# Per-head exponentials with the maximum as bias in a fused stack of eight parts, and the order lists that go with them

## What is computed

```python
x = x + tanh(g_xattn[0]) * L0_xattn(ctx, layernorm(x), mask, mask)   # l0a: 8 heads of 16, 64 keys, masked
x = x + tanh(g_ffn[0])   * L0_ffn(layernorm(x))      # l0f0, l0f1: two layers of local attention and GLU
x = x + tanh(g_xattn[1]) * L1_xattn(layernorm(x), ctx)               # l1a: product, patches picked by position
x = x + tanh(g_ffn[1])   * L1_ffn(layernorm(x))      # l1f: 8 experts of rank 16, top 2
x = x + tanh(g_xattn[2]) * L2_xattn(ctx, layernorm(x), mask)         # l2a: 8 heads of 16, 64 keys, masked
x = x + tanh(g_ffn[2])   * L2_ffn(layernorm(x))      # l2f, l2g: ternary weights, rounded activations
x = x + tanh(g_xattn[3]) * L3_xattn(layernorm(x), ctx)               # l3a: 16 heads of 8, 64 given and 64 own keys
x = x + tanh(g_ffn[3])   * L3_ffn(layernorm(x))      # l3f, l3g: ternary, convolution over 3 rows, silu
# in each of the two layers of L0_ffn:
q = l2norm(q) * qs; k = l2norm(k) * ksc; q, k = rotary_xpos(q, k)
attn = softmax(8 * q @ k.T, causal within 64 rows); o = attn @ v     # 8 heads of 64
```

## Time and profile before

| | us |
|---|---|
| median of 3 runs | 1541.98 (1537.93 to 1543.62) |
| the profiled execution | 1545.68 |
| its span | 1543.9 |
| TensorE, TensorE weight load busy | 1372.6, 951.6 |
| VectorE busy | 1358.0 |
| ScalarE busy | 1019.0 |
| GpSimd busy | 753.3 |

### The profile page before, as it was taken

How to read it: one execution, slowest core, us unless ns; L and a number is a source line. 1 busy time by engine, 2 the same in 40 slices (tenths; PEclk the granted TensorE clock), 3 DMA queues, 4 the chain that set the end, 5 groups by cost and what they waited for, 6 DMA issues and landing times.

```text
span 1543.9 us, 42177 instructions
## 1 busy us (share of the span) xinstructions
PE 1372.6 (89%) x16206; PEld 951.6 (62%) x16206; DVE 1358.0 (88%) x4054; ACT 1019.0 (66%) x2037; POOL 753.3 (49%) x1147
## 2 busy tenths in 40 slices
PE   4888999989999899998988999899899989998877
PEld 2557656666566666575666656576566666666644
DVE  5878999889988899998989898989899999998875
ACT  1465778676766666776766766776676677666554
POOL 6676354545635355446446435735544553552310
PEclk9999999999999999999999999999999999999978
DMA  7001211111101121111211111122111021110110
GB/s 224 10 15 52 71 22 29 29 46 45 41 18 38 45 45 46 35 38 31 62 26 43 44 32 45 21 55 47 33 41 38 21 58 37 36 41 19 52 30 6
DMA packets 131000, 64.38 MB, mean 42 GB/s; under 512 B 97642, under 2 KB 123626, under 8 KB 130545
## 3 DMA queue, kind: packets, MB, share of 16 engines
q1 hardware_dynamic: 128209, 56.56, 14.8%
q10 hardware_dynamic: 2592, 5.12, 0.9%
HBM read 50.06 MB, written 2.14 MB: 34 GB/s over the span
## 4 chain that ended last, share of the span: by engine, by line
PE 50%; DVE 23%; ACT 14%; POOL 7%; issue 4%; DMA 1%; SPq 1%; POOLq 1%; DVEq 0%
PE ps_all L1442 8%; PE ps_all L1506 4%; PE ps_all L1731 4%; PE ps_all L1565 4%; PE ps_all L1480 3%; DVE mx L1121 3%; PE ps_all L1435 3%; PE ps_all L1519 3%; ACT L814 2%; PE ps_all L1551 2%; POOL wide_a L601 2%; PE ps_all L1687 2%; DVE wide_b L1124 2%; POOL rden L601 2%; POOL rstd L601 2%
## 5 line engine op out<-in xcount | busy, mean ns | idle before, releaser
L601 POOL TENSOR_TENSOR rstd<-rstd,minus_half 128x1 f32<-128x1 f32 x320 | 187.4, 592 | 595.2 <-DVE rstd L1099 590.8
L601 POOL TENSOR_TENSOR rden<-rden,minus_half 128x16 f32<-128x16 f32 x64 | 190.8, 2981 | 9.4
L601 POOL TENSOR_TENSOR wide_a<-wide_a,wide_b 128x256 f32<-128x256 f32 x256 | 181.5, 740 | 0.5 <-DVE wide_b L1178 0.4
L1121 DVE TENSOR_REDUCE mx<-ps_all 128x8 f32<-128x512 f32 (+1 forms) x192 | 164.7, 860 | 18.4 <-PE ps_all L1468 6.0
L852 ACT COPY wide_a<-ps_all 128x512 f32<-128x512 f32 (+1 forms) x192 | 138.3, 727 | 58.6 <-PE ps_all L1442 33.5
L1442 PE MATMUL ps_all<-ident,wide_b 128*128 128x128 f32 x1024 | 156.3, 285 | 14.7 <-ACT wide_b L865 5.7
L1442 PEld LDWEIGHTS ps_all<-ident,wide_b 128*128 128x128 f32 x1024 | 117.0, 145 | 52.4 <-issue 15.7
L814 ACT ACT_TABLE_LOAD x115 | 147.5, 1283 | 2.0
L865 ACT ACTIVATE wide_b<-wide_b 128x512 f32<-128x512 f32 (+1 forms) x160 | 113.9, 715 | 47.4 <-DVE wide_b L1124 46.3
L1506 PE MATMUL ps_all<-w_qkv,ht_shift 128*128 128x512 f32 x256 | 125.7, 614 | 6.6 <-DVE wide_b L1124 3.3
L1124 DVE TENSOR_TENSOR wide_b<-ps_all,mx 128x512 f32<-128x512 f32 (+1 forms) x160 | 126.3, 790 | 2.1
(11 more groups left out here) (266 smaller groups left out, 3611.8 us busy)
## 6 DMA issues: line engine op xcount, KB each, us to landing
wide_a<-in_k SPq DMA_DIRECT2D x64, 256.0 KB, 3.2
wide_c<-wide_c SPq DMA_DIRECT2D x128, 64.0 KB, 2.2
v_pad<-in_v SPq DMA_DIRECT2D x32, 256.0 KB, 4.1
v_pair<-in_v SPq DMA_DIRECT2D x32, 136.0 KB, 2.7
ctx_t<-in_ctx_t SPq DMA_DIRECT2D x32, 128.0 KB, 2.7
ctx_s<-in_ctx SPq DMA_DIRECT2D x32, 128.0 KB, 3.2
xin<-in_x SPq DMA_DIRECT2D x32, 64.0 KB, 2.6
mask_row<-in_mask_f SPq DMA_DIRECT2D x32, 64.0 KB, 3.0
```

The costliest lines, as they stand in the source:

```text
L601: return gp.tensor_tensor(o, a, b, op)
L1121: v.tensor_reduce(most, of, AX.X, ALU.max).then_inc(*done(f"{n}_max"))
```

## The change

- In the four attentions of 64 keys the subtraction is gone. The maximum of each head, negated, is the bias of a per-head exponential that reads the scores' banks itself: eight instructions of 128x64 on ScalarE for one of 128x512. The banks' reader is now the exponential. For l0a the factor 0.25 moves into `w_tgt` and `b_q` in the setup.
- In the two layers only the keys are scaled by their norm. Queries are transposed unscaled from `wide_a` as soon as the rotation is added, and the queries' inverse norm is the scale of the exponential. A new stage `less` on VectorE multiplies maximum by inverse norm by -1 (128x8). GpSimd raises keys' and queries' sums apart (8 columns each), the queries' behind the rotation.
- `w_gate` and `w_a` are one tensor of 136 columns and one product. The value product of l3a is one over all 128 rows; the second batch's given rows are laid on the other half of the partitions, so the third load is four DMAs for two, and L1335 becomes two instructions.
- `ORDER` and `BANK_TABLE` are new throughout; their entries are left out here. The new lists hold 3442 turns for VectorE (3506 before), 704 for GpSimd (640), and the same number for the others.

```diff
--- before.py
+++ after.py
@@ STAGES, ORDER and BANK_TABLE @@
     "dve": """
-        l0a_st l0a_var l0a_eps l0a_y l0a_k l0a_qs l0a_max l0a_sub l0a_inv l0a_o l0a_x l0f_st l0f_var l0f_eps
-        l0f_y l0f0_den l0f0_turned l0f0_qkn l0f0_max l0f0_sub l0f0_inv l0f0_o l0f0_y1 l0f0_st l0f0_var
+        l0a_st l0a_var l0a_eps l0a_y l0a_k l0a_qs l0a_max l0a_inv l0a_o l0a_x l0f_st l0f_var l0f_eps l0f_y
+        l0f0_den l0f0_turned l0f0_qkn l0f0_max l0f0_less l0f0_inv l0f0_o l0f0_y1 l0f0_st l0f0_var l0f0_eps
...
     "pool": """
-        l0a_rstd l0a_part l0f_rstd l0f0n_rstd l0f0_rot l0f0_one l0f0_rstd l0f1n_rstd l0f1_rot l0f1_one
-        l0f1_rstd l1a_rstd l1f_rstd l2a_rstd l2f_rstd l2f_xb l3a_rstd l3f_rstd
+        l0a_rstd l0a_part l0f_rstd l0f0k_rstd l0f0_rot l0f0q_rstd l0f0_one l0f0_rstd l0f1k_rstd l0f1_rot
+        l0f1q_rstd l0f1_one l0f1_rstd l1a_rstd l1f_rstd l2a_rstd l2f_rstd l2f_xb l3a_rstd l3f_rstd
...
-l0a_sc 45621615304040511251022563062660 2 l0a_sub
+l0a_sc 62600365506204043053055032164333 2 l0a_exp
...
-l0f0_sc 45010523316401340640322422032363 2 l0f0_sub
+l0f0_sc 65530123065533541213200020503151 2 l0f0_exp
...
@@ -368,8 +368,8 @@
         g_init = sb("g_init", [P, D])
-        w_gate = sb("w_gate", [P, E])
-        w_a = sb("w_a", [P, E * R])
+        w_experts = sb("w_experts", [P, E * R + E])
+        w_a, w_gate = w_experts[:, 0:E * R], w_experts[:, E * R:E * R + E]
@@ -580,10 +580,12 @@
                     sp.wait_ge(signal("l3a1_pv", (i - VALUES) % G), reached("l3a1_pv", i - VALUES))
-                sp.dma_start(k_part[:, s].rearrange("p (n k) -> p n k", n=8)[:, :, 0:ROW], d["k3"][i]).then_inc(
-                    signal(f"third_in{s}"), 16)
-                sp.dma_start(v_pad[0:64, i % VALUES].rearrange("p b h e -> p (b h e)"), d["v3"][i]).then_inc(
-                    signal(f"third_in{s}"), 16)
+                for b in range(2):
+                    far_half = slice(ROW - ROW * b, P - ROW * b)
+                    sp.dma_start(k_part[:, s].rearrange("p (b j k) -> p b j k", b=2, j=4)[:, b, :, far_half],
+                                 d["k3"][i][:, 4 * b:4 * b + 4, :]).then_inc(signal(f"third_in{s}"), 16)
+                    sp.dma_start(v_pad[far_half, i % VALUES, b].rearrange("p h e -> p (h e)"),
+                                 d["v3"][i][:, HID * b:HID * b + HID]).then_inc(signal(f"third_in{s}"), 16)
@@ -750,6 +752,14 @@
                     tt(rstd[:, s:s + 1], rstd[:, s:s + 1], minus_half[:, 0:1], ALU.pow).then_inc(*done(f"{n}_rstd"))
+                def inv_norm(n, after, of):
+
+                    yield f"{n}_rstd"
+                    tile(after)
+                    gp.tensor_scalar(rden[:, s, of], den[:, s, of], 1e-24, None, ALU.max)
+                    gp.drain()
+                    tt(rden[:, s, of], rden[:, s, of], minus_half[:, of], ALU.pow).then_inc(*done(f"{n}_rstd"))
+
@@ -763,17 +773,14 @@
                     n = f"l0f{L}"
-                    yield f"{n}n_rstd"
-                    tile(f"{n}_den")
-                    gp.tensor_scalar(rden[:, s, :], den[:, s, :], 1e-24, None, ALU.max)
-                    gp.drain()
-                    tt(rden[:, s, :], rden[:, s, :], minus_half[:], ALU.pow).then_inc(*done(f"{n}n_rstd"))
+                    yield from inv_norm(f"{n}k", f"{n}_den", slice(8, 16))
...
                     n_op.then_inc(*done(f"{n}_rot"))
+                    yield from inv_norm(f"{n}q", f"{n}_den", slice(0, 8))
@@ -864,6 +871,17 @@
                         *done(f"{n}_exp"))
+
+                def exps64(n):
+                    yield f"{n}_exp"
+                    use(EXP_SET)
+                    tile(f"{n}_max")
+                    for h in range(8):
+                        m, j = h // 4, h % 4
+                        n_op = a.activation(wide_b[:, s, h * ROW:h * ROW + ROW],
+                                            pair_of_banks(f"{n}_sc", 256)[:, m, j * ROW:j * ROW + ROW], ACT.Exp,
+                                            bias=mx[:, s, 0, h:h + 1])
+                    n_op.then_inc(*done(f"{n}_exp"))
@@ -884,7 +902,15 @@
                     yield from move(f"{n}_qkt", f"{n}_qts", wide_a[:, s, :], ps(f"{n}_qkt"))
-                    yield from exps(n, BANK)
+                    yield f"{n}_exp"
+                    use(EXP_SET)
+                    tile(f"{n}_less")
+                    for h in range(8):
+                        c, m = h // 2, h % 2
+                        n_op = a.activation(wide_b[:, s, h * ROW:h * ROW + ROW],
+                                            pair_of_banks(f"{n}_sc", 256)[:, m, c * ROW:c * ROW + ROW], ACT.Exp,
+                                            scale=rden[:, s, h:h + 1], bias=mx[:, s, 0, 4 * m + c:4 * m + c + 1])
+                    n_op.then_inc(*done(f"{n}_exp"))
@@ -910,7 +936,7 @@
                 yield from move("l0a_yt", "l0a_ht", ht[:, s, :], ps("l0a_yt", 0, P))
-                yield from exps("l0a", BANK, 0.25)
+                yield from exps64("l0a")
@@ -927,7 +953,7 @@
                 yield from move("l2a_yt", "l2a_ht", ht[:, s, :], ps("l2a_yt", 0, P), scale=0.25)
-                yield from exps("l2a", BANK)
+                yield from exps64("l2a")
@@ -944,11 +970,12 @@
                 yield "l3a_vs"
-                act.wait_ge(signal(f"third_in{s}"), loaded(i, 32))
-                ends = v_pad[64:128, i % VALUES].rearrange("p b (n m) w -> p (b n) (m w)", m=2)
-                of = ps("l3a_qkv", BANK, 2 * D)[64:128].rearrange("p (n m e) -> p n m e", m=2, e=8)
-                for m in range(2):
-                    n = a.copy(ends[:, :, 48 * m:48 * m + 8], of[:, :, m])
+                act.wait_ge(signal(f"third_in{s}"), loaded(i, 64))
+                for b in range(2):
+                    half = slice(64 * b, 64 * b + 64)
+                    ends = v_pad[half, i % VALUES, b].rearrange("p (n m) (x e) -> p n (m x) e", m=2, e=16)
+                    of = ps("l3a_qkv", BANK, D)[half].rearrange("p (n m e) -> p n m e", m=2, e=8)
+                    n = a.copy(ends[:, :, 0:4:3, 0:8], of)
@@ -1016,8 +1043,10 @@
             dve.wait_ge(signal("gate_means"), 1)
-            stt(w_gate[:], ps_all[:, 1, 0:E], -1.0 / D, w_gate[:], ALU.mult, ALU.add)
-            stt(w_a[:], ps_all[:, 2, 0:E * R], -1.0 / D, w_a[:], ALU.mult, ALU.add)
+            ts(w_tgt[:], w_tgt[:], 0.25, None, ALU.mult)
+            ts(b_q[:], b_q[:], 0.25, None, ALU.mult)
+            stt(w_gate, ps_all[:, 1, 0:E], -1.0 / D, w_gate, ALU.mult, ALU.add)
+            stt(w_a, ps_all[:, 2, 0:E * R], -1.0 / D, w_a, ALU.mult, ALU.add)
@@ -1179,13 +1208,21 @@
                     yield f"{n}_qkn"
-                    tile(f"{n}n_rstd")
+                    tile(f"{n}k_rstd")
                     tile(f"{n}_rot")
-                    tt(wide_b[:, s, :].rearrange("p (g e) -> p g e", g=16),
-                       wide_a[:, s, :].rearrange("p (g e) -> p g e", g=16),
-                       bc(rden[:, s, :], 2, ROW), ALU.mult).then_inc(*done(f"{n}_qkn"))
-                    yield from less_max(n, pair_of_banks(f"{n}_sc", 256).rearrange("p m (c k) -> p m c k", c=4),
-                                        wide_b[:, s, 0:BANK].rearrange("p (c m k) -> p m c k", c=4, m=2))
+                    tt(wide_b[:, s, BANK:2 * BANK].rearrange("p (g e) -> p g e", g=8),
+                       wide_a[:, s, BANK:2 * BANK].rearrange("p (g e) -> p g e", g=8),
+                       bc(rden[:, s, 8:16], 2, ROW), ALU.mult).then_inc(*done(f"{n}_qkn"))
+                    most = mx[:, s, 0, :].rearrange("p (m c) -> p m c", m=2)
+                    yield f"{n}_max"
+                    tile(f"{n}_sc")
+                    v.tensor_reduce(most, pair_of_banks(f"{n}_sc", 256).rearrange("p m (c k) -> p m c k", c=4), AX.X,
+                                    ALU.max).then_inc(*done(f"{n}_max"))
+                    yield f"{n}_less"
+                    tile(f"{n}_max")
+                    tile(f"{n}q_rstd")
+                    stt(most, most, -1.0, rden[:, s, 0:8].rearrange("p (c m) -> p m c", m=2), ALU.mult, ALU.mult
+                        ).then_inc(*done(f"{n}_less"))
@@ -1222,8 +1259,11 @@
                 def scores64(n):
-                    return less_max(n, pair_of_banks(f"{n}_sc", 256).rearrange("p m (j k) -> p m j k", j=4),
-                                    wide_b[:, s, 0:BANK].rearrange("p (m j k) -> p m j k", m=2, j=4))
+                    yield f"{n}_max"
+                    tile(f"{n}_sc")
+                    v.tensor_reduce(mx[:, s, 0, :].rearrange("p (m j) -> p m j", m=2),
+                                    pair_of_banks(f"{n}_sc", 256).rearrange("p m (j k) -> p m j k", j=4), AX.X, ALU.max,
+                                    negate=True).then_inc(*done(f"{n}_max"))
@@ -1331,10 +1371,12 @@
                 tile("l3a_q")
-                dve.wait_ge(signal(f"third_in{s}"), loaded(i, 32))
-                tt(k_part[:, s].rearrange("p (b j k) -> p b j k", b=2, j=4)[:, :, :, ROW:P],
```

(77 more changed lines are left out.)

256 lines of the change are left out of this document (104 added, 152 removed).

## The result

The changed kernel takes 1591.56 us (1585.45 to 1591.66, three runs) where the kernel before takes 1541.98: 1.030 of it, 95% interval 1.027 to 1.033. It is 50 us slower. 1509 was forecast, with a range of 1480 to 1546, so both the sign and the range were wrong.

A forecast was written before the change was run, and what follows sets the result against it. TensorE (89% busy) and VectorE (88%) were taken to bound the kernel together. TensorE work -18, fill +2 and the plateau's idle time -17 made -33 us: span 1511, run 1513, median 1509, range 1480 to 1546.

The forecast's parts named there:

- DVE: VectorE's busy time: dropped subtractions and keys-only scaling, less small additions, take it from 1358 to 1256 us.
- ACT: ScalarE's busy time: eight exponentials for one add 191 us, fewer table loads save 5; from 1019 to 1205 us.
- PE: TensorE's work: the merged products save 16.7 to 21.9 us, taken as 18, giving 1354; called the surest part.
- POOL, SP, the fill: GpSimd's split powers add 45 us (798), nothing or a few tenths in time; SP's third loads nothing; fill +2 us.
- Latency and banks: Each attention's path grows 0.42 or 0.87 us, 2.6 us a tile, not seen with over five tiles in flight.
- rival B: Slower: TensorE stands for score banks held until the exponentials, at most 195 us plus ACT's queue; 1574 to 1607; chance 0.11.
- On the plateau PE at 93% instead of 91.7%: TensorE's busy share between 140 and 1400 us rises, shortening the plateau from 1242 to 1225, -17 us; chosen, not measured.
- Added waits: New waits on ScalarE, VectorE and TensorE, with other tiles' work behind them: put at nothing, bound 45 us.
- A: Rival: no gain, the chain's mixture of engines decides, +8 or -11 us; 1531 to 1550; chance 0.17.
- C: Rival: VectorE was what held TensorE, plateau goes to 95%, -43 rather than -17 us; median 1483; chance 0.17.
- D: Rival: only TensorE's own saving shows, -18 to -22 us, 1520 to 1526; chance 0.55 together with the forecast.

The follow-up runs named there:

- late_work: one_exp with five or six useless 128x64 exponentials on ScalarE behind each exponential's signal, so weights and banks come early while ScalarE stays loaded: 1608.16 us, 1.042.
- no_sub: Kernel before without the subtraction in the 64-key attentions, one row maximum as bias of one exponential, 13 ScalarE turns moved earlier: 1627.16 us, 1.054.
- small_sub: Kernel before with the subtraction in the 64-key attentions cut from 128x512 to 128x8 from the ninth tile on: 1535.42 us, 0.996.
- one_exp: Changed kernel with one 128x512 exponential, using the first head's bias and scale, instead of eight in all 128 attentions of 64 keys: 1521.95 us, 0.985.
- merged_only: Kernel before with only the two merged products and the four third loads of the change: 1542.3 us, 1.000.
- shared-maximum kernels: One row maximum as bias of one exponential, no subtraction: 1607.21 us in the changed kernel's lists; in the old lists 1627.16, with merged products 1615.63.

## Why the prediction was wrong

**DVE.** Forecast 1256, measured 1277.9. The new terms were right (0.686 for 0.704, 0.211 for 0.221, 0.417 for 0.419). The miss of 22 us is mostly in how busy time is counted. Added up by group, VectorE is busy 1575.5 us before and 1495.8 after, 26 of the latter from overlapping records of the setup: 106 us less, near the 102 forecast. The busy line counts overlapping records once (1358), so an instruction taken out of a dense row gives up less busy time than its own length: without the 128 subtractions (87 us) the line falls by 66 (1292.3), while shortening 96 of them by 44 us lowers it by 45 (1313.3).

**ACT.** Forecast 1205, measured 1187.1, with 0.346 and 0.426 us for 0.312 and 0.408. One exponential is longer than forecast, but eight in a row are as long as forecast (1.75 and 2.48 us), since they overlap more. The size of this term was right. Its price in time was the error.

**PE.** Forecast 1354, measured 1375.3. By group the merged products save 21 us, as forecast (l1f_lg 26.3 to 14.5, l3a_qkv's values 21.7 to 12.4). The surplus lies in groups that were not touched: the transposes of L1484 last 293 ns, 285 before, and the mean granted clock is 0.963, 0.980 before. By the prediction's own 14 us for each 1% of the clock this is 24 us, which would explain the surplus of 21. With one exponential the clock is 0.972 and PE 1341.3, or some 1362 with the missing records. The saving of 18 us was put on the path because TensorE was the fullest engine; alone it gave 0.0 us (-4 to +4). TensorE stands for others in its fixed order 8% of the plateau, and shorter work only lengthened that.

**POOL, SP, the fill.** 773.9 for 798: the powers of eight columns last 1.70 us, as forecast, and the 320 powers of one column went from 187.4 to 178.2 us. Waits on the queries' norm are 0.7 us in all (L1224), nothing. Third loads: nothing seen. The fill: 1009 matmuls at 140 us in both.

**Latency and banks.** The bank waits on the exponentials are small in the changed kernel (14.1 us on PE, against 65 for a third of rival B), and late_work shows the whole loss without either. But "not seen" is too strong for the latency: PE's waits for the exponentials in front of the line that turns the weights grew from 5.7 to 28.1 us. In no_sub, where the table was not made anew, PE's waits for the exponential are far larger.

**The sum: the step that failed.** "On the plateau PE at 93% instead of 91.7%." It came out at 89.4%. The step weighed a relieved VectorE against a fuller ScalarE by asking which engine is fullest. At 80% ScalarE was counted as having room. With it failed the term "Added waits": it names what then happened, exponentials on ScalarE with other tiles' copies behind them for which PE waits, and puts nothing, but its reason and its bound of 45 us are about VectorE only. PE's waits for ScalarE grew by 50 us. The runs give the two prices: VectorE's relief 0.13 us per us (small_sub), ScalarE's load 0.40 us per us (70 for 177, one_exp), 0.46 in the layers, 0.47 for useless work (86 for 183, late_work). For -102 us of VectorE that is -13, for +177 of ScalarE +70: together +57, where +50 was measured. (With one exponential 22 us of gain are left for VectorE's relief, the products and the new order together, where these prices give 13.) The chain's shares were not these prices either: 23% for VectorE and 14% for ScalarE, which went to 30% as the work grew.

**Rivals.** A used the chain's shares and ended at 1531 to 1550; its engine was the right one, its price of ScalarE's work (+39 us at most) half of what was measured. B gave the right size (1574 to 1607) by luck: late_work has the whole loss with the banks given back early. C and D are refuted, C by 0.13 us per us, D by merged_only. The sentence that held is the last: TensorE was made idle where the old order did not, by exponentials on ScalarE, for which it waited itself or which stood in front of copies that it needed.

**Why ScalarE's work is so dear at 75%.** What the runs show: it costs as occupancy, whether TensorE then waits for the exponentials (changed kernel) or for the copies behind useless ones (late_work), and the layers' eight cost more a us (0.46) than those of l0a and l2a (0.2). The layers' eight are longer, 2.48 against 1.75 us, and also stand at another place of a tile's path; which of the two makes them dearer is open. That a long stretch in one piece, with copies of other tiles queued behind, is why, fits the timeline at 703.91; it was argued from there and not tried, for instance by parting the eight into two turns of four.

**What stays open.** Whether 1592 is the best order for this work. The new order reaches 1522 once ScalarE is relieved, so it isn't a poor order in itself, but no list was fitted to the variants. The shared-maximum kernels do less work than either kernel in total (ScalarE 1021 to 1028 us, VectorE 1292 to 1299) and ran only in lists made for other work; whether they would beat 1542 with an order and banks of their own was not tried. No run that computes the whole reference was faster than the kernel before.

## What to carry to other kernels

In a kernel with in-order queues fitted to each other, do not price a moved us by which engine is fullest: here ScalarE at 66% cost 0.40 us a us, and VectorE at 88% gave back 0.13. A probe can measure such a price before the change is built, with useless work added to one engine behind its signals, or work shortened in place. Splitting one instruction into eight to save a pass on another engine is paid on the engine that serves everyone's copies. And where the order is fitted, an edit tried in the old order shows the misfit first: 87 us of work removed made this kernel 5% slower.
